# Local attention layers: values projected once per token and laid out by blocks through a DRAM buffer, x turned earlier, Gelu later

## What is computed

```python
def shift_tokens(t):      # the second half of the features comes from the token before
    a, s = jnp.split(t, 2, -1)
    s = jnp.pad(s, ((0, 0), (1, 0), (0, 0)))[:, :-1]
    return jnp.concatenate([a, s], -1)

def look(t):              # every block of 32 tokens sees itself and the block before
    p = jnp.pad(t, ((0, 0), (0, 0), (1, 0), (0, 0), (0, 0)))
    return jnp.concatenate([p[:, :, :nw], p[:, :, 1:]], axis=3)
...
q, k, v = jnp.split(x @ Wqkv, 3, -1)            # 16 heads of 64, inner width 1024
q = l2norm(q) * qs; k = l2norm(k) * ksc         # then the rotary turn of both
sim = jnp.einsum('bhwie,bhwje->bhwij', bq, look(bk)) * QK_SCALE
attn = jax.nn.softmax(jnp.where(mask, -max, sim), -1)
out = jnp.einsum('bhwij,bhwje->bhwie', attn, look(bv))
x = out.reshape(b, n, 1024) @ Wo + x
...
a, gate = jnp.split(layernorm(shift_tokens(x)) @ W1 + b1, 2, -1)
x = a * gelu(gate) @ W2 + b2 + x
```

## Time and profile before

| what | value |
|---|---|
| median of three runs | 7447.41 us |
| the profiled execution | 7455.9 us |
| its span, first to last instruction | 7454.2 us |
| the stage of the local layers | about 2246 to 6492 us of the span |
| busy share of the span: TensorE, VectorE, ScalarE, GpSimd | 90%, 69%, 56%, 33% |
| mean granted TensorE clock | 0.941 of full |

### The profile page before, as it was taken

One profiled execution on the slowest core, in us unless ns is written; L12 is line 12 of the kernel. 1 busy time (PEld: TensorE's weight loads), 2 busy tenths in 40 slices (PEclk: granted clock), 3 DMA queues, 4 the chain that ended last, 5 costly groups with the idle time before them and its releaser, 6 DMA issues. The chain is left out here.

```text
span 7454.2 us, 217712 instructions
## 1 busy us (share of the span) xinstructions
PE 6733.5 (90%) x79314; PEld 4586.7 (62%) x79314; DVE 5166.1 (69%) x14566; ACT 4157.2 (56%) x9934; POOL 2490.2 (33%) x2527
## 2 busy tenths in 40 slices
PE   7999979999988888888888888888888888869998
PEld 5777657776655555555555555555555555557666
DVE  4555445555657777777877777778777777758378
ACT  4666637774235555555555555555555555536455
POOL 0000010000005555555555555555555555430030
PEclk9999979999989999999999999999999999979989
DMA  1000000000010000000000000000000000010210
GB/s 33 24 25 24 29 22 29 27 28 19 9 42 27 4 4 4 22 4 4 4 22 5 4 4 22 4 5 4 22 4 4 23 4 4 5 35 16 73 43 24
DMA packets 131939, 133.17 MB, mean 18 GB/s; under 512 B 40302, under 2 KB 121982, under 8 KB 130814
## 3 DMA queue, kind: packets, MB, share of 16 engines
q1 hardware_dynamic: 115454, 103.45, 4.3%
q0 software_dynamic: 7936, 24.28, 1.1%
q10 hardware_dynamic: 8448, 4.20, 0.2%
HBM read 55.48 MB, written 10.49 MB: 9 GB/s over the span
## 5 line engine op out<-in xcount | busy, mean ns | idle before, releaser
L932 POOL TENSOR_TENSOR l_rot<-l_rot,l_by_sin 128x512 f32<-128x512 f32 x768 | 961.1, 1272 | 586.8 <-DVE l_by_sin L1290 578.5
L1007 PE MATMUL bank<-w_w,l_x 128*128 (+1 forms) x1536 | 892.0, 692 | 218.4 <-ACT l_x L1181 202.8
L1286 DVE TENSOR_TENSOR l_rot<-bank,l_cos 128x512 f32<-128x512 f32 x768 | 520.1, 677 | 687.8 <-ACT l_squares L1188 687.5
L939 POOL TENSOR_TENSOR l_rot<-l_rot,l_norms 128x512 f32<-128x512 f32 x768 | 798.7, 1070 | 485.5 <-DVE l_norms L1311 485.5
L1188 ACT ACTIVATE l_squares<-bank 128x512 f32<-128x512 f32 x768 | 447.6, 596 | 518.7 <-DVE l_square_sums L1295 491.3
L1013 PE MATMUL bank<-w_w,l_x_windows 128*128 (+1 forms) x1536 | 721.0, 602 | 0.0
L946 POOL TENSOR_TENSOR l_probs<-l_probs,l_inverse 128x512 f32<-128x512 f32 x384 | 392.2, 1042 | 893.0 <-DVE l_inverse L1333 893.0
L486 PE MATMUL bank<-a_qk 64*128 64x256 f32 (+2 forms) x2660 | 680.1, 381 | 6.1 <-DVE a_qk L668 3.5
L1023 PE MATMUL bank<-ident,l_rot 128*128 128x128 f32 x3072 | 550.0, 327 | 93.0 <-ACT l_probs_t L1209 75.3
L1007 PEld LDWEIGHTS bank<-w_w,l_x 128*128 128x128 f32 x1536 | 257.0, 196 | 528.1 <-issue 522.9
L593 ACT ACTIVATE a_probs_t<-bank 128x512 f32<-128x512 f32 (+1 forms) x656 | 355.9, 554 | 354.1 <-PE bank L494 354.1
(11 more groups left out here) (264 smaller groups left out, 14459.2 us busy)
## 6 DMA issues: line engine op xcount, KB each, us to landing
a_x<-normed_t SPq DMA_DIRECT2D x320, 128.0 KB, 2.0
l_stage_rows<-inner SPq DMA_DIRECT2D x98, 128.0 KB, 2.1
w_w<-in_w SPq DMA_DIRECT2D x6, 2048.0 KB, 9.6
l_shifted_half<-inner SPq DMA_DIRECT2D x98, 63.5 KB
f_w<-in_f SPq DMA_DIRECT2D x9, 514.5 KB
a_w<-in_a POOLq DMA_DIRECT2D x18, 256.0 KB, 2.9
f_w<-in_f POOLq DMA_DIRECT2D x9, 512.0 KB
c_x<-normed_t SPq DMA_DIRECT2D x36, 128.0 KB, 2.0
```

What stands on the lines that cost most here:

```text
L932: nc.gpsimd.tensor_tensor(rot[s][n][:], rot[s][n][:], by_sin[n % 2][:], ALU.add).then_inc(summed, 1)
L939: nc.gpsimd.tensor_tensor(mine, mine, along(norms[s][:, 8 * n:8 * n + 8], HD), ALU.mult)\
L1007: nc.tensor.matmul(rows_p[i][:], x[:, W + i * P:W + (i + 1) * P], layer_w(layer, quad * QUAD, QUAD), start=True, stop=True).then_inc(rows_ ...
L1286: nc.vector.tensor_tensor(rot[s][2 * a + i][:], rows_p[i][:], cos[:, i, :], ALU.mult)
```

## The change

Values are projected once per token: `project_v` multiplies the unwindowed `x` (two matmuls of 512 columns in a half), ScalarE moves them to `v_rows` (two moves), SyncE stores them to a buffer in DRAM (`store_v`) whose first 32 rows are zero, and loads them back in overlapping blocks with four transfers (`load_v`) once `weigh` has read the old ones. `weigh` waits for them (`v_loaded`). Both halves now project the values of unit `h + 2`, an iteration ahead. `copy_window` and `x_windows` are gone.

The order changes too. `turn_x` and `move_x` move from the end of the odd half to its middle, so `gates` has to wait until `move_x` has emptied `f_p`. `open_gates` moves behind `move_qk`, `ups` behind `weigh`, and one `Square` of a single column (`warm`) follows the last Gelu. SyncE waits for `heads_filled` between a store and the loads of a half. The core of the diff:

```diff
-        x, x_windows = sb("x", [P, W + SEQ]), sb("x_windows", [P, 4, 2, 2, W])
+        x, v_rows = sb("x", [P, SEQ]), sb("v_rows", [P, 2, QUAD])
+        v_dram = [nc.dram_tensor(f"{name}_values{o}", (W + SEQ, QUAD), F32, kind="Internal").ap() for o in range(2)]
...
+                def store_v(u, o, fill):
+                    for i in range(2):
+                        sp.wait_ge(t_freed[i], fill + 1)
+                        sp.sem_inc(begun, 1)
+                    sp.dma_start(v_dram[o][W:, :].rearrange("(i p) n -> p i n", p=P), v_rows[:]).then_inc(v_stored, DMA)
+
+                def load_v(u, o):
+                    sp.wait_ge(v_stored, (u + 1) * DMA)
+                    sp.sem_inc(begun, 1)
+                    for i in range(2):
+                        for s in range(2):
+                            at = i * P + s * W
+                            sp.dma_start(v[HD * i + W * s:HD * i + W * (s + 1), :, o * QUAD:(o + 1) * QUAD],
+                                         v_dram[o][at:at + P, :].rearrange("(j c) n -> c j n", c=W)).then_inc(v_loaded[o], DMA)
+
+                def iteration(g, L=None, last=False):
                     sp.wait_ge(f_filled, 4 * g + 2)
                     sp.sem_inc(begun, 1)
                     sp.wait_ge(ffn_added, g + 6)
                     sp.sem_inc(begun, 1)
                     stage_x(g + 2)
+                    if not last:
+                        send_v(g, 0)
                     sp.wait_ge(normed, g + 1)
                     sp.sem_inc(begun, 1)
                     sp.wait_ge(added, g + 2)
                     sp.sem_inc(begun, 1)
                     shift((g + NB - 1) & (NB - 1))
+                    if L is not None:
+                        sp.wait_ge(ffn_added, NB * L + 19)
+                        sp.sem_inc(begun, 1)
+                        sp.dma_start(fw[:], t["f2"][bass.ds(L + 1, 1), :, :].rearrange("a p n -> p (a n)"))\
+                            .then_inc(fw_loaded, DMA)
+                    if not last:
+                        send_v(g, 1)
+
+                def send_v(g, o):
+
+                    h = 2 * g + o
+                    sp.wait_ge(v_loaded[o], (g + 1) * 4 * DMA)
+                    sp.sem_inc(begun, 1)
+                    store_v(h + 2, o, t_fill(h))
+                    sp.wait_ge(heads_filled, 4 * h + 4)
+                    sp.sem_inc(begun, 1)
+                    load_v(h + 2, o)
...
-                def copy_window(f):
-                    pool.wait_ge(x_moved, f + 1)
-                    pool.sem_inc(begun, 1)
-                    for s in range(2):
-                        part = x[:, s * W:s * W + SEQ].rearrange("p (t j c) -> p j t c", t=2, c=W)
-                        last = nc.gpsimd.tensor_copy(x_windows[:, :, :, s, :], part)
-                    last.then_inc(window_ready, 1)
...
                 def project_v(o, fill, layer):
-                    for j in range(4):
-                        reached(pe, t_freed[j % 2], fill + j // 2)
-                        nc.tensor.matmul(t_p[j % 2][:], x_windows[:, j].rearrange("p t s c -> p (t s c)"),
-                                         layer_w(layer, wv_at + o * QUAD, QUAD), start=True, stop=True)\
-                            .then_inc(t_filled[j % 2], 2)
+                    for i in range(2):
+                        reached(pe, t_freed[i], fill)
+                        nc.tensor.matmul(t_p[i][:], x[:, tile_of(i)], layer_w(layer, wv_at + o * QUAD, QUAD), start=True,
+                                         stop=True).then_inc(t_filled[i], 2)
...
                     pe.wait_ge(masked, 2 * h + 2)
+                    pe.wait_ge(v_loaded[o], ((h >> 1) + 1) * 4 * DMA)
                     pe.sem_inc(begun, 1)
...
                 def gates(g):
                     pe.wait_ge(fw_loaded, ((g + NB - 2) >> 4) * DMA + DMA)
+                    if not isinstance(g, int) or g < LAST:
+                        pe.wait_ge(x_moved, g + 3)
                     hide(g, 1, 0)
...
                         h = 2 * g + o
                         fill, more = t_fill(h), o == 0 or not last
-                        turned = fill + 2 if more else fill
+                        turned = fill if last else fill + 1
                         if not last:
                             if o == 0:
                                 pe.wait_ge(x_moved, g + 2)
@@ -1140,25 +1178,22 @@
                         scores(h, o)
                         if not last:
                             project_rows(h + 2, o, 1, (g + 1) >> 4)
+                            project_v(o, fill, (g + 1) >> 4)
                         if o == 0:
-                            project_v(1, fill, g >> 4)
                             output(g)
                             give(g)
                         elif more:
-                            pe.wait_ge(window_ready, g + 2)
-                            project_v(0, fill, (g + 1) >> 4)
+                            turn_x(g + 2, 3 * g + 2)
                         if o == 1:
                             gates(g)
                         turn_probs(h, turned)
                         if more:
-                            turn_qk(h + 1, 1 - o, fill + 3)
+                            turn_qk(h + 1, 1 - o, turned + 1)
                         if o == 0:
                             turn_normed(g)
-                        else:
+                        weigh(h, o, turned)
+                        if o == 1:
                             ups(g)
-                        weigh(h, o, turned)
-                    if not last:
-                        turn_x(g + 2, 3 * g + 3)
...
-                def move_v(o, j, fill):
-                    act.wait_ge(t_filled[j % 2], 2 * (fill + j // 2 + 1))
-                    nc.scalar.activation(v[:, j, o * QUAD:(o + 1) * QUAD], t_p[j % 2][:], ACT.Copy).then_inc(t_freed[j % 2], 1)
+                def move_v(u, i, fill):
+                    act.wait_ge(t_filled[i], 2 * (fill + 1))
+                    if i == 0:
+                        reached(act, v_stored, u * DMA)
+                    nc.scalar.activation(v_rows[:, i, :], t_p[i][:], ACT.Copy).then_inc(t_freed[i], 1)
...
+                        if not last:
+                            move_v(h + 2, 0, fill)
+                            move_v(h + 2, 1, fill)
+                        exps(h, 0)
+                        exps(h, 1)
+                        if o == 1 and not last:
+                            move_x(g + 2, f_fill(g) + 1)
+                        move_probs(fill if last else fill + 1)
                         if more:
-                            move_v(1 - o, 0, fill)
-                            move_v(1 - o, 1, fill)
-                        exps(h, 0)
-                        if more:
-                            move_v(1 - o, 2, fill)
-                        exps(h, 1)
-                        if more:
-                            move_v(1 - o, 3, fill)
-                        if o == 1:
-                            open_gates(g)
-                        move_probs(fill + 2 if more else fill)
-                        if more:
-                            move_qk(1 - o, fill + 3)
+                            move_qk(1 - o, fill + 1 if last else fill + 2)
                         if o == 0:
                             move_normed(g)
+                        else:
+                            open_gates(g)
+                            nc.scalar.activation(warm[:], core.ones[:, 0:1], ACT.Square)
                         move_heads(h, o)
-                    if not last:
-                        move_x(g + 2, f_fill(g) + 3)
```

More of the change, by code:

```diff
@@ L834, in local_layers @@
         normed_rows, normed_t = sb("normed_rows", [P, 2, D]), sb("normed_t", [P, SEQ])
+        warm = sb("warm", [P, 1])
         gate, hidden = sb("gate", [P, 3, SEQ]), sb("hidden", [P, 3, SEQ])
@@ L844, in t_fill, with hidden_fill @@
         def t_fill(h):
-            return 5 * h + 4
+            return 4 * h + 4 if not isinstance(h, int) or h <= 2 * LAST else 8 * LAST + 7
         def f_fill(g):
             return 4 * g + 2 if not isinstance(g, int) or g <= LAST else 4 * LAST + 2 + 3 * (g - LAST)
+        def hidden_fill(g):
+            return f_fill(g) + (2 if not isinstance(g, int) or g < LAST else 1)
         def rows_of(b):
@@ L907, in load_layer, with layer @@
                         .then_inc(w_loaded, DMA)
+                def layer(L):
+                    with sp.Fori(0, 2) as m:
+                        iteration(NB * L + m)
+                    iteration(NB * L + 2, L)
+                    load_layer(L)
                 load_scales(0)
                 stage_x(0)
+                sp.wait_ge(cleared, 2)
+                for o in range(2):
+                    sp.dma_start(v_dram[o][0:W, :], heads_t[0:W, 0:2, :].rearrange("p a n -> p (a n)")).then_inc(v_cleared, DMA)
+                sp.wait_ge(v_cleared, 2 * DMA)
                 shift(NB - 2)
@@ L913, in _ @@
                 stage_x(1)
```

(41 more changed lines are left out.)

33 lines of the change are left out of this document (13 added, 20 removed).

## The result

| | before | changed |
|---|---|---|
| device time, us (median, range) | 7446.67 (7445.31 to 7449.09) | 7328.33 (7327.24 to 7335.66) |
| ratio (95% interval) | | 0.9843 (0.9826 to 0.9860) |
| span profiled, mean granted clock | 7454.2, 0.941 | 7326.5, 0.953 |

The change is faster by 118 us, 1.6%. The forecast was 170 us faster, 7280; 7328 lies inside its range.

A forecast was written before the change was run, and what follows sets the result against it. It took no single engine as the bound, but a chain through the engines from `rotate` to `rotate`. At full clock 41.45 us plus 1.1 of clock gave period 42.6; (44.39 - 42.6) x 95 = 170 us off 7447.4: 7280, range 7165 to 7405.

The forecast's parts named there:

- The chain: Steps across the engines through both halves of a local-layer iteration; 19.6 + 21.85 = 41.45 us a period at full clock.
- O: Start of `rotate` in the odd half, from which the odd half's step times are counted.
- E to O: Even half, from its `rotate` to the odd half's: 19.6 us forecast, against 19.98 before.
- projection: Odd half, the next projection after `ups`: starts at O + 18.7, with no `move_x` between.
- next E: Start of `rotate` in the following even half: O + 21.85 at full clock.
- The wait for normed rows: Even half: `turn_normed` waits for VectorE's normed rows, from `turn_qk`'s end at E + 14.2 to E + 15.2.
- VectorE's idle time: Before the even `rotate`: down from 6.6 to some 4 us, split with its wait for `ups`.
- The clock: TensorE's half clock after the longer gap before `gates`: 1.1 us a period, making the period 42.6.
- 2.4: Half clock on both `gates` and `turn_qk`, in us: period 43.85, 7396 us; as a rival 17%.
- rival of full clock: Low clock falls where it costs nothing: 279 us gained, 7168 us; 15%.
- transfers at nothing: Value stores and loads, 3 MB an iteration, taken as hidden by some 40 us of iteration: cost nothing.
- slip of 3 us of the weights: Feed-forward weights, needed once a layer at O + 9.3, late behind SyncE's added issues: 18 us in all.

The follow-up runs named there:

- `filler7`: The changed kernel with seven idle matmuls, results unused, between `turn_x` and `gates`, where TensorE waits: 7199.60 us, ratio 0.9666.
- `fw_first`: The changed kernel with the feed-forward weights' transfer issued before `shift` in SyncE's list instead of behind it: 7311.79 us, ratio 0.9816.
- `x_early_only`: The changed kernel with `turn_x` and `move_x` still early, but Gelu back before `move_probs` and `ups` before `weigh`: 7267.38 us, ratio 0.9758.
- `x_before_exps`: The changed kernel with `move_x` placed ahead of the two exponentials: 7197.82 us, ratio 0.9662.
- `v_only`: Value path and transfers of the change, but x, Gelu and `ups` ordered as in the kernel before, no `warm`: 7479.19 us, ratio 1.0042.
- `warm_exp`: The changed kernel with the one-column Square (`warm`) made an Exp: 7238.21 us, ratio 0.9719.
- `no_warm`: The changed kernel with the one-column Square (`warm`) taken out: 7336.05 us, ratio 0.9843.

## Why the prediction came out as it did

**The chain was right.** At full clock, step by step, in us from O (the second column that of the 41.30 iteration, the third that of the common iteration shown, whose low stretch is on `gates`):

| | forecast at full clock | 41.30 iteration | common iteration |
|---|---|---|---|
| E to O | 19.6 | 19.38 | 19.38 |
| `gates` | 9.3 | 9.18 | 9.18 |
| `turn_probs` | 10.6 | 10.55 | 11.88 |
| `turn_qk` | 11.9 | 11.83 | 13.31 |
| `ups` | 17.4 | 17.29 | 18.77 |
| projection | 18.7 | 18.78 | 20.31 |
| next E | 21.85 | 21.92 | 23.45 |

E to O ended a little earlier, at VectorE's own 19.4, as in the earlier trace rows. The wait for normed rows, E + 14.2 to 15.2 in the forecast, is 0.86 us, and `weigh` starts at E + 15.5, forecast 15.6. VectorE's idle time is where I had it too low: its 6.62 us before the even `rotate` are 2.25 there and 4.5 before `ups`, together 6.7 in the common iteration and 5.2 in the 41.30 one, against some 4 in the forecast.

**The clock** cost 1.2 or 1.5 us in nearly every iteration, forecast 1.1: by turns on `gates`, and on `turn_probs` with a part of `turn_qk`. That 1.1 came close is partly luck: it was a choice between nothing and 2.4, for which I pointed at an iteration that pays nothing, and what happened is that nearly every iteration pays about half. `filler7` shows the cause: with the gap filled, and the order the same, the low stretch is gone. My rival of full clock (7168) is what `filler7` comes to (7199.6), but for the first period and the six with new weights, which hold 28 us more than the usual ones. The Trainium skill (TensorE: Matmul & The Clock Gate, "HAM oscillation") says that each burst behind a wait starts cold. This trace agrees in part: in 90 of 94 periods the work behind the gap has a low stretch. But it doesn't cover the burst, in about half the iterations `gates` itself runs at full clock (4072.56, 1.10 us), and in four, with the same gap of 3.52 us, nothing is low. The whole 2.4 us was not paid in the usual periods. What decides between these cases no run here shows.

**The mis-sized term: transfers at nothing.** I wrote that even a slip of 3 us of the weights would be 18 us in all, and left it out of the sum. The wait is 6.2 us each time (37.0 / 6) where 3.5 were due: a slip of 2.7, and 16.5 us in all by `fw_first`. The bound was right, and the term belonged in the sum. The row that I had is SyncE's issue of the shift in before, 2.6 us; I did not ask what it takes with a megabyte queued: 5.1 us. Besides, the first period is 49.9 us (45.9 before, 44.0 without transfers) and the loop starts 3.6 us later (2275.1 against 2271.5).

**The sum again,** from the traces: the mean period fell by 44.39 − 42.95 = 1.45 (unrounded), 136 us in 94 periods. Of this 2.2 are the chain where the clock costs nothing (43.5 to 41.3). Against it stand some 0.5 of clock (before lost 44.39 − 43.5 = 0.9 a period; the change loses about 1.35, what `filler7` gives back), 0.2 of weights and 0.1 for the long first period. I had 42.6 where 42.95 was measured: 33 us of the 52 missing. Three terms were too low, the weights by some 17 us, the clock by some 24 (1.35 against 1.1 a period) and the first period by some 7; the chain came out 0.15 us shorter than forecast, which hid 14 of them. 3.6 us is the later start, 5 lie behind the loop (the last load is 132.6 us earlier, the end 127.7). The last 9 are no cost: the profiled execution of before was 9 us above its median, that of the change at its median.

**What I had not seen** is how much of the clock's cost depends on the order. Before paid it in two iterations of three (its low head comes free), the values alone in each, the change in nearly each, `x_early_only` in two of three, `x_before_exps` hardly ever. The 44.39 that I started from held 0.9 us of clock, more than half of what the clock takes from the change; in the earlier trace rows I saw both kinds of iteration and did not count them.

## What to carry to other kernels

Look at the distances of one instruction from iteration to iteration before using their mean; where they fall into two kinds, compare the granted clock in a window of each. An order that closes a gap of TensorE, or idle matmuls in it, can be worth more than the work removed (131 and 129 us here, against 118 for the whole change). This loop ended with Gelu's table and began with another's, and the load stood at its head, on the path; one small activation of the other table (an Exp, not a Square) at the end moved it off. A new stream of transfers is priced by what its issues and queues do to the small ones behind it as well as by its bytes.

## What the runs showed of the hardware

- Less work gained nothing in the steady loop: `v_only` with two matmuls fewer in each half has 44.4 us a period, all at a low clock for part of it (0.89 in the stage), against 43.5 and 44.8 before.
- SyncE's issue of the shift's small transfer (L884) took 5.1 us behind queued value loads, against 2.6 in before and 2.7 without them; the landing of `l_stage_rows`, 128 KB, went from 2.1 to 4.6 us and back to 2.0 without them, with the DMA engines only a third busy.
- A table load (1283 ns) stands before the first Square of each iteration, and with `warm_exp` it is gone from the head once the loop ends in an Exp. The Square at the end has no load, and without it (`no_warm`) the time is the same. The Trainium skill (ScalarE: Activation LUTs, "Table sets: the hidden batching unit") says that cheap functions are in every set; its examples are relu, copy, identity and abs. If Square is one of them, as I took it in the prediction, the Square at the end agrees, and the load at the head isn't there for the Square itself; what it is there for no run here shows.
